# Attention B on one core: k turned and split ahead of q, a score bank per head in the short tiles, chunk rounding behind them

## The reference, cut to what matters

```
q, k, v = dequant(x, qw_q), dequant(x, qw_k), dequant(x, qw_v)   # 32, 8, 8 heads of 128
q, k = rope(q), rope(k)
scores = q @ k.T / sqrt(128), causal, softmax
out = dequant(softmax @ v, qw_o)      # weights: (int4 - 8) * scale per 128 rows
```

## Time and profile before

| | |
|---|---|
| median of 3 executions | 1515.82 us (1514.83 to 1516.57) |
| profiled execution | 1517.17 us, its span 1515.4 us |
| TensorE busy | 1447.4 us, 96% of the span |
| VectorE, ScalarE, GpSimd busy | 1228.2 (81%), 874.5 (58%), 253.0 us (17%) |
| mean granted TensorE clock | 0.995 of full |
| step 0 of group 0 begins | 580.77 us |
| group 2, from tile 2's scores to those of group 3 | 820.13 to 928.76 us |
| in that stretch TensorE, VectorE, ScalarE, GpSimd busy | 105.60, 94.13, 66.21, 23.46 of 108.63 us |

### The profile page before, as it was taken

One profiled execution on the slowest core, in us unless ns is written; L12 is line 12 of the kernel. 1 busy time (PEld: TensorE's weight loads), 2 busy tenths in 40 slices (PEclk: granted clock), 3 DMA queues, 4 the chain that ended last, 5 costly groups with the idle time before them and its releaser, 6 DMA issues.

```text
span 1515.4 us, 24024 instructions
## 1 busy us (share of the span) xinstructions
PE 1447.4 (96%) x8164; PEld 720.0 (48%) x8164; DVE 1228.2 (81%) x2578; ACT 874.5 (58%) x1474; POOL 253.0 (17%) x193
## 2 busy tenths in 40 slices
PE   5999999999999997999999999999999999999898
PEld 3453333333332454555555555555555555555454
DVE  3698888888884587888898888887988888878954
ACT  2247777777678134665665665665665655756631
POOL 3312000000000222212212212212212212111011
PEclk8999999999999999999999999999999999999999
DMA  3894000000001253576675675675674675643541
GB/s 100 146 139 132 1 0 0 0 0 0 0 1 20 57 139 93 121 152 136 129 143 133 126 150 132 128 150 125 135 160 107 135 153 121 137 93 71 99 74 56
DMA packets 351757, 143.70 MB, mean 95 GB/s; under 512 B 314680, under 2 KB 324408, under 8 KB 351648
## 3 DMA queue, kind: packets, MB, share of 16 engines
q1 hardware_dynamic: 351664, 142.50, 44.9%
HBM read 58.66 MB, written 6.19 MB: 43 GB/s over the span
## 4 chain that ended last, share of the span: by engine, by line
PE 76%; DVE 15%; ACT 5%; issue 3%; DMA 0%; SPq 0%; DVEq 0%; ACTq 0%
PE ps L1597 10%; PE ps L1599 10%; PE ps L1598 10%; PE ps L1352 8%; PE ps L1405 8%; PE ps L1391 7%; PE ps L1556 4%; PE ps L1678 3%; PE ps L1680 3%; PE ps L1679 3%; DVE mx L899 2%; DVE nmr L1101 2%; PE ps L1519 2%; PE ps L1284 2%; DVE hl L1118 2%
## 5 line engine op out<-in xcount | busy, mean ns | idle before, releaser
L729 ACT ACTIVATE x<-ps,nmb,factor 128x128 f32<-128x128 f32 (+7 forms) x256 | 211.4, 831 | 289.1 <-DVE nmb L1103 289.1
L899 DVE TENSOR_REDUCE mx<-ps 128x1 f32<-128x512 f32 x512 | 326.9, 686 | 50.5 <-PE ps L1352 48.3
L637 ACT ACTIVATE proj<-ps 128x1024 f32<-128x1024 f32 x256 | 248.3, 1021 | 98.5 <-PE ps L1391 97.6
L1118 DVE SCALAR_TENSOR_TENSOR hl<-x,rden,hl 128x128 f16<-128x128 f32 (+7 forms) x256 | 208.1, 813 | 8.9 <-ACT hl L737 8.4
L737 ACT ACTIVATE hl<-x,rden 128x128 f16<-128x128 f32 (+7 forms) x256 | 184.1, 767 | 25.2 <-DVE rden L1114 24.4
L1101 DVE TENSOR_REDUCE nmr<-ps 128x1 f32<-128x128 f32 (+7 forms) x256 | 191.9, 750 | 3.3 <-PE ps L1661 2.4
L534 POOL TENSOR_TENSOR tmp<-tmp 128x640 f32<-128x640 f32 x64 | 98.5, 1539 | 514.4 <-DVE tmp L1097 514.4
L1352 PE MATMUL ps<-ks,qs 96*128 (+1 forms) x512 | 181.3, 383 | 2.4 <-DVE mx L899 1.0
L1597 PE MATMUL ps<-wh,xTh 128*128 128x256 f16 (+1 forms) x512 | 166.8, 326 | 0.0
L1598 PE MATMUL ps<-wl,xTh 128*128 128x256 f16 (+1 forms) x512 | 166.8, 326 | 0.0
L1599 PE MATMUL ps<-wh,xTl 128*128 128x256 f16 (+1 forms) x512 | 166.8, 326 | 0.0
(11 more groups left out here) (173 smaller groups left out, 2199.2 us busy)
## 6 DMA issues: line engine op xcount, KB each, us to landing
scale<-sp_n SPq DMA_DIRECT2D x32, 384.0 KB, 4.4
st<-in_L_attn_b_qw_q_dram SPq DMA_DIRECT2D x32, 256.0 KB, 2.8
st<-in_L_attn_b_qw_o_dram SPq DMA_DIRECT2D x32, 256.0 KB, 2.9
scale<-so_n SPq DMA_DIRECT2D x32, 256.0 KB, 3.5
qs<-scratch SPq DMA_DIRECT2D x18, 256.0 KB, 9.4
hlT<-hl SPq DMA_TRANSPOSE x256, 3.4
scratch<-pieces SPq DMA_DIRECT2D x5, 768.0 KB, 8.6
xnat<-attn_a_hidden_state_dram SPq DMA_DIRECT2D x8, 256.0 KB, 5.1
```

What stands on the lines that cost most here:

```text
L637: nc.scalar.activation(pbuf[:, e % 4, :].rearrange("p (b n) -> p b n", b=2), ps[:, b:b + 2, :], ACT.Exp, scale=float(HD) ** -0.5).then_inc ...
L729: nc.scalar.activation(pr[:, h, 0:n], flat(2 * (h % 2), n), ACT.Exp, bias=nmb[:, h:h + 1], scale=factor[:, par, 0:1], accum_out=den[:, h:h ...
L899: nc.vector.tensor_reduce(mx[:, f, k // 2, k % 2:k % 2 + 1], ps[:, bank(k), :], AX.X, ALU.max).then_inc(s_mx, 1)
L1118: nc.vector.scalar_tensor_tensor(hl[:, h, n:2 * n], pr[:, h, 0:n], rden[:, h:h + 1], hl[:, h, 0:n], ALU.mult, ALU.subtract).then_inc(s_lo, 1)
```

## The change

On TensorE `turn_b` turns k first and signals it (`s_kT`), then q. On ScalarE `turned` rounds k first, then q; in steps 1 to 3 `high_part` stands behind `turned` and no longer ahead of it. On VectorE `turned` makes kTl first and then qTl in two instructions of two heads each. TensorE begins head 0's scores of the next tile when k and the first half of q are there, and waits for the second half ahead of the projection. In tiles 0 to 3, where a head's scores fit one bank, each head has a bank of its own (`score_bank`); the scores then wait for the exponential of the same head a step before (tiles 1 to 3), or for no exponential of their own step (tile 0). From tile 4 on banks and waits are as before. In group 0 products that only keep TensorE busy are moved and are other in number.

```diff
@@ -224,6 +224,10 @@
         def v_slot(t, par):
 
             return t if t > 1 else t + T * par
+
+        def score_bank(t, h):
+
+            return (0, 2, 1, 3)[h] if t < T // 2 else 2 * (h % 2)
 
         def k_slot(t, par):
 
@@ -314,6 +318,7 @@
         s_rpa = sem("s_rpa")
         s_vl = sem("s_v_lo")
         s_vb = sem("s_vb")
+        s_kT = sem("s_k_turned")
         s_qkT = sem("s_qkT")
         s_qke = sem("s_qke")
         s_sc = sem("s_sc")
@@ -698,11 +703,12 @@
                                      scale=HEADROOM / (XSCALE * WSCALE)).then_inc(s_vb, 1)
 
             def turned(v, t, par):
+                c = k_slot(t, par) * P
+                act.wait_ge(s_kT, v + 1)
+                nc.scalar.activation(kTh[:, c:c + P], ps[:, 7, 0:P], ACT.Copy,
+                                     scale=HEADROOM / (XSCALE * WSCALE)).then_inc(s_qke, 1)
                 act.wait_ge(s_qkT, v + 1)
                 nc.scalar.activation(qTh[:, t % 2].rearrange("p h n -> p (h n)"), ps[:, 6, :], ACT.Copy,
-                                     scale=HEADROOM / (XSCALE * WSCALE)).then_inc(s_qke, 1)
-                c = k_slot(t, par) * P
-                nc.scalar.activation(kTh[:, c:c + P], ps[:, 7, 0:P], ACT.Copy,
                                      scale=HEADROOM / (XSCALE * WSCALE)).then_inc(s_qke, 1)
 
             def context_high(g, t):
@@ -726,7 +732,7 @@
                         act.wait_ge(s_nat[h], 64)
                         act.wait_ge(s_xh, 2 * T + 2 * h + 2)
                     act.wait_ge(s_nb, u * R + h + 1)
-                    nc.scalar.activation(pr[:, h, 0:n], flat(2 * (h % 2), n), ACT.Exp, bias=nmb[:, h:h + 1],
+                    nc.scalar.activation(pr[:, h, 0:n], flat(score_bank(t, h), n), ACT.Exp, bias=nmb[:, h:h + 1],
                                          scale=factor[:, par, 0:1], accum_out=den[:, h:h + 1]).then_inc(s_eb, 1)
 
                 def high(h):
@@ -753,9 +759,11 @@
                 values(u + 1, par if t < T - 1 else 1 - par, t2)
                 high(0)
                 high(1)
-                if not last:
+                if not last and not 1 <= t <= 3:
                     high_part(g + 1, t, 1 - par)
                 turned(u + 1, t2, par if t < T - 1 else 1 - par)
+                if not last and 1 <= t <= 3:
+                    high_part(g + 1, t, 1 - par)
                 exponentials(2)
                 exponentials(3)
                 if exists(*before(g, t, 1)):
@@ -1098,7 +1106,7 @@
 
             def maximum(u, h, n, par):
                 dve.wait_ge(s_sc, u * R + h + 1)
-                nc.vector.tensor_reduce(nmr[:, h:h + 1], flat(2 * (h % 2), n), AX.X, ALU.max, negate=True).then_inc(s_mxb, 1)
+                nc.vector.tensor_reduce(nmr[:, h:h + 1], flat(score_bank(n // P - 1, h), n), AX.X, ALU.max, negate=True).then_inc(s_mxb, 1)
                 dve.wait_ge(s_mxb, u * R + h + 1)
                 nc.vector.tensor_scalar(nmb[:, h:h + 1], nmr[:, h:h + 1], factor[:, par, 0:1], None,
                                         ALU.mult).then_inc(s_nb, 1)
@@ -1120,13 +1128,16 @@
 
             def turned(v, t, par):
 
-                dve.wait_ge(s_qke, v * 2 + 2)
-                nc.vector.scalar_tensor_tensor(qTl[:, t % 2].rearrange("p h n -> p (h n)"), ps[:, 6, :],
-                                               HEADROOM / (XSCALE * WSCALE), qTh[:, t % 2].rearrange("p h n -> p (h n)"),
-                                               ALU.mult, ALU.subtract).then_inc(s_ql, 1)
                 c = slice(k_slot(t, par) * P, (k_slot(t, par) + 1) * P)
+                dve.wait_ge(s_qke, v * 2 + 1)
                 nc.vector.scalar_tensor_tensor(kTl[:, c], ps[:, 7, 0:P], HEADROOM / (XSCALE * WSCALE), kTh[:, c],
                                                ALU.mult, ALU.subtract).then_inc(s_ql, 1)
+                dve.wait_ge(s_qke, v * 2 + 2)
+                for h in range(0, R, 2):
+                    nc.vector.scalar_tensor_tensor(qTl[:, t % 2, h:h + 2, :].rearrange("p h n -> p (h n)"),
+                                                   ps[:, 6, h * P:(h + 2) * P], HEADROOM / (XSCALE * WSCALE),
+                                                   qTh[:, t % 2, h:h + 2, :].rearrange("p h n -> p (h n)"),
+                                                   ALU.mult, ALU.subtract).then_inc(s_ql, 1)
 
             def add(v, t, par):
                 dve.wait_ge(s_op, v + 1)
@@ -1257,7 +1268,7 @@
                     elif phase == 2 and t >= 2:
                         pe.wait_ge(s_xl, t - 1)
                     elif phase == 3 and t < 2:
-                        pe.wait_ge(s_ql, G * T * 2)
+                        pe.wait_ge(s_ql, G * T * 3)
                     elif phase == 3 and t in (4, 5):
                         pe.wait_ge(s_eb, G * T * R)
                     for k in range(KC):
@@ -1617,9 +1628,9 @@
             def turn_b(v):
                 pe.wait_ge(s_rpa, v + 1)
                 pe.wait_ge(s_vl, v + 1)
-                for h in range(BH):
-                    dst = ps[:, 6, h * P:(h + 1) * P] if h < R else ps[:, 7, 0:P]
-                    ins = nc.tensor.transpose(dst, rc1[:, h * P:(h + 1) * P], ident[:])
+                nc.tensor.transpose(ps[:, 7, 0:P], rc1[:, R * P:BH * P], ident[:]).then_inc(s_kT, 1)
+                for h in range(R):
+                    ins = nc.tensor.transpose(ps[:, 6, h * P:(h + 1) * P], rc1[:, h * P:(h + 1) * P], ident[:])
                 ins.then_inc(s_qkT, 1)
 
             def output(v, heads, par):
@@ -1645,11 +1656,13 @@
             def keys(g, t, h, par):
                 u = g * T + t
                 n = (t + 1) * P
-                if h >= 2:
+                if 1 <= t < T // 2:
+                    pe.wait_ge(s_eb, u * R + h + 1 - R)
+                elif h < 2 and exists(*before(g, t, 1)):
                     pe.wait_ge(s_eb, u * R + h - 1)
-                elif exists(*before(g, t, 1)):
+                elif h >= 2 and t >= T // 2:
                     pe.wait_ge(s_eb, u * R + h - 1)
-                b = 2 * (h % 2)
+                b = score_bank(t, h)
                 for c in range(0, n, 512):
                     w = min(512, n - c)
                     at = c + (k_slot(t, par) * P if par else 0)
@@ -1687,10 +1700,9 @@
                 last = isinstance(g, int) and g == G - 1
                 end = last and t == T - 1
                 one, two = before(g, t, 1), before(g, t, 2)
-                if g == 0 and t == 1:
-                    keep_busy(3, wbT, 512)
-                pe.wait_ge(s_ql, u * 2 + 2)
+                pe.wait_ge(s_ql, u * 3 + 2)
                 keys(g, t, 0, par)
+                pe.wait_ge(s_ql, u * 3 + 3)
                 if not end:
                     project_all(u + 1, *after(g, t), par if t < T - 1 else 1 - par)
                 keys(g, t, 1, par)
@@ -1701,15 +1713,18 @@
                     tokens(3, 0, 1)
                 if exists(*two):
                     output_second(*two, par if t >= 2 else 1 - par)
-                if g == 0 and t <= 1:
-                    keep_busy(3, wbT, 512)
-                    keep_busy(3, wbT, 256)
                 early = R // 2 if t == 0 and exists(*one) else 0
                 if early:
                     values(*one, 1 - par, 0, early)
                 keys(g, t, 3, par)
+                if g == 0 and t <= 1:
+                    pe.wait_ge(s_xl, T)
+                    for _ in range(2):
+                        keep_busy(4, wbT, 512)
                 if not end:
                     turn_b(u + 1)
+                    if g == 0 and t == 0:
+                        keep_busy(4, wbT, 512)
                 else:
                     tokens(3, 2, 3)
                 if exists(*one):
```

## The result

The changed kernel takes 1520.16 us (median of 8, 1518.71 to 1520.9) against 1515.32 for the kernel before on the same chip (8 runs, 1513.78 to 1517.22). The ratio is 1.0029 with a 95% interval of 1.0020 to 1.0038: slower by 4.8 us (3.0 to 5.8). The forecast was 1522.1, slower by 6.3. The profiled execution took 1518.88 us, its span is 1517.0 us.

A forecast was written before the change was run, and what follows sets the result against it. TensorE bounds attention B, but in steps 1 to 3 a chain through the other engines sets the pace. Six inner groups +6.7, group 0 about 0, last group −0.4: +6.3 us, 1522.1 us; range 1512 to 1526.5.

The forecast's parts named there:

- Tile 2 comes 0.96 earlier: Step 1 of an inner group: TensorE starts tile 2's scores 0.96 us earlier, at 819.17 instead of 820.13.
- GpSimd's subtraction meets L1118 and holds it to its end: Steps 1 to 3: L539 holds VectorE's product L1118; price per step is L539's shift, 0.74, then 0.64 us.
- What reaches VectorE's later work: Inner group: addition into xnat 0.74 us later; rotations of steps 2, 3 and 4 0.27, 0.82 and 1.46 late.
- Tiles 3 and 4: TensorE starts tile 3 0.50 us early, tile 4 0.66 late; head 3's scores in step 4 cost 0.36 more.
- The rest of the group: Steps 5 and 6 add some 0.1 us; an inner group loses 1.1 together, six groups +6.7.
- Group 0: Loses the same but starts about 0.5 us earlier, with no addition into xnat in its first steps: about 0.
- Group 7: Last group, without L539: gains 0.5 us at tile 2, about 0.9 by tile 4, half given back: −0.4.
- the upper end of +10.5: Top of the forecast's own range, 1526.5 us: L539 or the halves 0.1 us dearer in each of 18 steps.
- The banks: A score bank per head: worth 0 by itself; without it waits for the exponentials would cut the earlier starts.
- The halves: VectorE's low part of q in two instructions of 256 columns, 0.34 us each: 0.07 us more for the pair.
- The second: Rival: no hold in steps 1 to 3, steps just become shorter; −7.2 us, 1508.6 us; chance 0.10.
- The first: Rival: in steps 1 to 3 only the inversion is held, L1118 isn't; −2.4 us, 1513.4 us; chance 0.14.
- The third: Rival: the hold is there but TensorE hardly feels it, VectorE's room being 0.3 wider; 0 to +3 us; chance 0.16.

The follow-up runs named there:

- Kernel 5: The changed kernel with GpSimd's subtraction of chunks 1 to 3 beside the next rotation and the chunk rounding ahead of k and q again; 1507.64 us.
- kernel 4: The changed kernel with GpSimd's subtraction of chunks 1 to 3 put off to the next step, beside VectorE's rotation; 1508.26 us.
- Kernel 3: The changed kernel with GpSimd's subtraction of chunks 1 to 3 cut to 16 of 768 columns, for groups 1 to 6; 1510.80 us.
- kernel 7: The changed kernel with the subtraction beside the rotation and q's low part in one instruction again; 1511.68 us.
- kernel 12: The changed kernel with the subtraction beside the rotation, the old pairs of banks and waits, and group 0's filler products where they were before; 1511.68 us.
- kernel 2: The kernel before with only the chunk rounding moved behind ScalarE's copies of q and k in steps 1 to 3; 1524.23 us.
- kernel 8: The changed kernel with the subtraction beside the rotation and the old pairs of banks and waits, keeping the new fillers; 1514.53 us.

## Why the prediction was right, point by point

- **Tile 2 comes 0.96 earlier.** From step 1's rotation (812.63) to tile 2's scores it is 5.80 us for 6.76: 0.96. Kernel 5 against kernel 4 (6.29 for 5.79) shows that only half of this, 0.50, is the move's; the rest is k ahead of q and the halves.
- **GpSimd's subtraction meets L1118 and holds it to its end.** The step had them at 5.95 and 6.00 us after the rotation; they came at 5.98 and 5.99. Kernel 3 shows the hold to be the cause. Had VectorE come first, the forecast gave about the same price; GpSimd was first in all seven groups, so the trace doesn't decide that case. One reading behind this step was too strong: rows 6 and 7 show VectorE's two products 1.29 us longer but GpSimd's two only 0.46, less than one whole product of VectorE. The rule of the Trainium skill ("SBUF — State Buffer", Who interferes with whom), that the second to start is blocked until the first has finished, is what the trace shows on VectorE's side (1.91 for 0.47) and in kernel 4 on GpSimd's (2.02 for 1.64).
- **What reaches VectorE's later work.** The addition into xnat was to come 0.74 later and came 0.77 later (8.10 us after the rotation for 7.33). The rotations of steps 2, 3 and 4 were to be 0.27, 0.82 and 1.46 late; from step 1's rotation they are 0.30, 0.85 and 1.46 late (11.71, 24.12 and 37.24 for 11.41, 23.27 and 35.78).
- **Tiles 3 and 4.** Tile 3 was to start 0.50 early and starts 0.49 early; tile 4 was to be 0.66 late, waiting for head 2's exponential, and is 0.77 late, waiting for it. Head 3's scores of tile 4 follow those of head 2 after 2.43 us for 2.16, 0.27 more where 0.36 was forecast.
- **The rest of the group.** In group 2, from which it was worked out, 1.1 us was forecast and 1.10 measured. The forecast took the same for six groups, and that was too much. Cut where each group's tile 0 starts, groups 1 to 3 lose 1.16, 1.11 and 1.11, groups 4 to 6 only 0.81, 0.89 and 0.76: 5.8 in all (653.5 to 659.4) and not 6.7. In the kernel before, TensorE waits 0.70, 0.44 and 0.17 ahead of value products in step 0 of those three groups (for what, the profile doesn't name), in the changed one 0.42, 0.21 and not at all, so part of the lateness goes into waits that were there. What the forecast also didn't have is the place of the loss: it put a new wait ahead of head 3's scores in step 4, and the timeline shows two more at the turns of steps 2 and 3, for v's low part, 0.94 and 0.77 us. They are where the lateness of VectorE comes to TensorE; the sum, worked out along VectorE's chain, had it without the name.
- **Group 0** was put at 0 and gave +0.2 (106.33 to 106.52 from its tile 0 to that of group 1; the −0.8 of the table has the 0.96 of group 1's tile 2 in it). That it came out near 0 is in part luck, as the reasons given were only half right. The hold costs group 0 1.8 us, near the 1.9 of an inner group, so the missing addition into xnat saves next to nothing, and the rest of the change gives 1.6 there, against 0.8 in an inner group (kernel 4, 104.72 us): the halves have 0.8 of it and the banks with the shifted fillers 1.7 (kernels 7 and 12, to tile 2 of group 1). **Group 7** was put at −0.4 and gave −0.6: −2.3 by the spans, of which the clock is some 1.7. So +0.2 + 5.8 − 0.6 is 5.4 for the 6.3 of the sum; the measured 4.8 has an interval of 3.0 to 5.8, and the forecast is a little above it. Of the range, the upper end of +10.5 isn't reached by the term named for it: 0.1 in each of 18 steps is 1.8 us.
- **Costed at nothing.** The banks were put at 0 by themselves, which no run tested (none adds them alone to the kernel before), with the remark that without them the early starts would be cut by waits for the exponentials; that is what kernels 2 and 12 show, and with the fillers they are worth 3.4 us. The halves were put at 0.07 us a step of cost; against q's low part in one instruction they are a gain of 1.7 us by the traces and 3.4 by the medians: whole, the low part ends 0.27 later and TensorE waits for all of it. Neither shows in the sum, because the 0.96 of tile 2 was worked out with both in place.
- **The rivals.** The second, no hold anywhere, gave 1508.6; kernel 4, which is the changed kernel without the hold, takes 1508.3. So that arithmetic was right and its condition wrong, by parts too: −5.4 in groups 1 to 6 for −5.0, −1.6 in group 0 for −1.8, −0.6 in group 7 for −0.4. The first fell with the 1.91 us. The third (0 to +3) fell too, though the interval's lower end, 3.0, touches it: of 3.5 us held in a group (1.44 + 1.14 + 0.95) 1.9 reach TensorE (109.90 against 108.03).

## What to carry to other kernels

Before an instruction is moved for the sake of its consumer, follow everything that it releases to the engine where that runs, and lay it over the other engines' work there: here ScalarE's rounding was free to move and the GpSimd subtraction behind it was not. Where VectorE and GpSimd both read SBUF, give the GpSimd work to a stretch in which VectorE reads one operand from PSUM; here it cost nothing there. And a move that brings one consumer forward in a loop gains only if it also shortens the way to the next turn of the loop: check which queue entries lie ahead of that way in both orders.

## What the runs showed of the hardware that was not expected

- The start that decides can be 0.01 us apart: at 818.61 and 818.62 VectorE lost the whole 1.44 us, and so it was in all seven groups. In step 1 a shift of VectorE's work by a few hundredths could give the other order; no run tried it.
- A two-element instruction on SBUF was held and a one-element one wasn't. In kernel 4, VectorE beside GpSimd's addition (810.26, 1.54 us):

```profile
810.55 0.21 DVE L1116 TENSOR_SCALAR nmb<-nmr,factor 128x1 f32<-128x1 f32 x1
...
811.49 0.34 DVE L1124 TENSOR_SCALAR rden<-den 128x2 f32<-128x2 f32 x1 [0.72 <-ACT x L740]
```

  The first has its mean of 0.21 us in the middle of the addition; the second takes 0.34 for 0.17 and ends at 811.83, 0.03 after GpSimd's record. They differ in their operands as well as in their count, so which of these decides is open.
- Two waits of 2.2 to 2.4 us on TensorE in the first steps of attention B were each followed by some 3 us at half the clock, where waits of 0.9 to 1.0 us in the same places weren't (kernels 8 and 12). The length of a single wait doesn't decide it alone: just before attention B's steps TensorE waits 0.93 and 1.02 us in the changed kernel and in the kernel before alike, and only the changed one had some 3 us at half the clock behind them.
